# Windowed attention: two of a tile's three weighted rows added on GpSimd before TensorE transposes and sums

## The reference, cut to what matters

```python
kv_c = kv @ w_kv_comp                       # 32 latent channels per key
qc = q @ w_q_down
q_nope, q_rope = (qc @ w_q_up), _rope(qc @ w_q_rope)      # 16 heads x 64 each
k_nope, v = (kv_c @ w_k_up), (kv_c @ w_v_up)
k_rope = _rope(kv_c @ w_k_rope)
scores = (q_nope . k_nope + q_rope . k_rope) * scale
good = (k_idx <= q_seg) & (k_idx >= q_seg - LOOKBACK)     # LOOKBACK = 2
attn = softmax(where(good, scores, neg))
out = attn @ v, heads joined, @ w_out
```

## Time and profile before

| what | us |
|---|---|
| median of 3 runs (lowest, highest) | 1641.42 (1634.97, 1651.33) |
| profiled execution | 1648.7 |
| span of its trace | 1647.0 |
| this phase's steady part, from the first rotation to the end of the tail | 50.20 to 223.77 |

### The profile page before, as it was taken

The page is one execution under the profiler, slowest core; times in us unless marked ns, Lnnn a source line. Parts: engine busy times, 40 slices in busy tenths (PEclk is TensorE's granted clock), DMA queues, the critical chain, the costliest instruction groups (busy, mean ns, idle before and its releaser), DMA issues. The chain is left out here.

```text
span 1647.0 us, 23707 instructions
## 1 busy us (share of the span) xinstructions
PE 1427.8 (87%) x9151; PEld 726.4 (44%) x9151; DVE 982.5 (60%) x1768; ACT 688.9 (42%) x1204; POOL 630.3 (38%) x628
## 2 busy tenths in 40 slices
PE   6868786988989999899968999899999877899984
PEld 3345453333334444444334444444445333355642
DVE  4798948677731222468556774745455344578866
ACT  2444432666642000257534773244433432355522
POOL 1587734354222221333123312534421312356662
PEclk7989997889988999869987998899999978979996
DMA  3000010000020000100001002000000010000000
GB/s 109 0 1 1 1 47 1 1 1 1 1 81 0 1 0 0 53 2 1 11 1 53 2 2 47 1 2 1 1 2 2 2 30 1 7 1 2 2 1 28
DMA packets 17238, 20.65 MB, mean 13 GB/s; under 512 B 7819, under 2 KB 13179, under 8 KB 16488
## 3 DMA queue, kind: packets, MB, share of 16 engines
q1 hardware_dynamic: 17128, 19.13, 3.8%
HBM read 17.94 MB, written 1.05 MB: 12 GB/s over the span
## 5 line engine op out<-in xcount | busy, mean ns | idle before, releaser
L1823 DVE CUSTOM_DVE_ANT_0 P<-P,L2f_mask 128x128 f32<-128x128 f32 (+3 forms) x256 | 118.5, 521 | 105.6 <-PE P L1715 105.6
L1020 DVE TENSOR_REDUCE L0f_nm<-P 128x2 f32<-128x768 f32 (+3 forms) x88 | 97.7, 1120 | 44.4 <-PE P L917 44.1
L1999 PE MATMUL P<-L0m_hm,L0m_w 128*128 128x512 f32 x256 | 113.3, 602 | 0.0
L1793 ACT ACTIVATE L2f_prob<-P 128x1024 f32<-128x1024 f32 x80 | 80.6, 1025 | 74.0 <-PE P L1727 74.0
L974 ACT ACTIVATE L0f_prob<-P 128x512 f32<-128x512 f32 x160 | 87.1, 605 | 39.9 <-PE P L928 38.5
L1634 POOL TENSOR_SCALAR_AFFINE_SELECT L2f_prob<-L2f_prob 128x512 f32<-128x512 f32 x64 | 40.0, 638 | 165.6 <-ACT L2f_prob L1793 165.6
L1715 PE MATMUL P<-L2f_ks,L2f_qs 48*128 48x512 f32 (+3 forms) x512 | 91.8, 471 | 0.3 <-DVE L2f_nm L1823 0.3
L1727 PE MATMUL P<-L2f_qs,L2f_ks 49*128 49x256 f32 (+3 forms) x512 | 84.5, 444 | 3.1 <-DVE L2f_nm L1823 2.3
L2402 POOL TENSOR_TENSOR L3x_exm<-L3x_exm,L3x_rec 128x2048 f32<-128x2048 f32 x16 | 72.4, 4524 | 27.0 <-DVE L3x_rec L2588 27.0
L871 POOL TENSOR_SCALAR_AFFINE_SELECT L0f_prob<-L0f_prob 128x512 f32<-128x512 f32 x64 | 39.9, 638 | 101.9 <-ACT L0f_prob L974 95.0
L1999 PEld LDWEIGHTS P<-L0m_hm,L0m_w 128*128 128x128 f32 x256 | 49.4, 194 | 60.7 <-issue 60.7
(11 more groups left out here) (577 smaller groups left out, 3347.5 us busy)
## 6 DMA issues: line engine op xcount, KB each, us to landing
L0m_w<-in_L0m_w SPq DMA_DIRECT2D x1, 2048.0 KB, 7.9
L0f_va<-in_L0f_va SPq DMA_DIRECT2D x3, 512.0 KB, 4.5
in_xt<-in_x SPq DMA_DIRECT2D x1, 1024.0 KB
L0x_segi<-in_segb SPq DMA_DIRECT2D x1, 1024.0 KB, 5.2
L0m_w<-in_L0m_w SPq DMA_DIRECT2D x1, 1024.0 KB, 9.9
out<-out_o SPq DMA_DIRECT2D x4, 256.0 KB, 2.4
L1x_va<-in_va SPq DMA_DIRECT2D x3, 256.0 KB, 3.2
L1x_vr<-in_vr SPq DMA_DIRECT2D x3, 256.0 KB, 4.1
```

The costliest lines, as they stand in the source:

```text
L1020: nc.vector.tensor_reduce(S.nm[:, qt, first:first + 2 * many].rearrange("p (i e) -> p e i", e=2), P[:, bank:bank + 2, 0:many * width].rear ...
L1793: nc.scalar.activation(S.prob_of(b, g)[:, at:at + 2, :], P[:, bank:bank + 2, :], ACT.Exp).then_inc(*S.act_done.up())
L1823: m = nc.vector.tensor_tensor_reduce(out=at, in0=at, in1=mask[:, T - width:T], scale=1.0, scalar=-3.0e38, op0=ALU.add, op1=ALU.max, accum_ ...
L1999: m = mm(P[:, slot(b, i) + part, :], w1[:, e, part * 512 + i * 128:part * 512 + i * 128 + 128], hm[b % 2][:, e, :], start=e == 0, stop=e = ...
```

## The change

On POOL, L1189 signals a new semaphore `weighed`, POOL waits for it, and adds row 1 of the tile to row 0 in place (128x512); that add now gives the signal for which TensorE and ACT wait. TensorE turns rows 0 and 2 alone: 8 matmuls a tile in place of 12. All three rows are still computed by L1189.

```diff
         ops.tensor_tensor(pv[t % 2][:], kg[b % 3][:, qt, :, 0:32].unsqueeze(2).to_broadcast([128, 3, H, 32]),
-                          p[b % 2][:, qt].unsqueeze(3).to_broadcast([128, 3, H, 32]), ALU.mult)\
+                          p[b % 2][:, qt].unsqueeze(3).to_broadcast([128, 3, H, 32]), ALU.mult).then_inc(*weighed.up())
+        eng.wait_ge(weighed.sem, t + 1)
+        ops.tensor_tensor(pv[t % 2][:, 0], pv[t % 2][:, 0], pv[t % 2][:, 1], ALU.add)\
             .then_inc(*(S.vals_pool if S.pool_has(s) else S.vals_dve).up())
...
+    weighed = ph.count("weighed")
...
                     for g in range(4):
-                        for j in range(3):
+                        for j in (0, 2):
                             m = mm(P[:, bank, g * 128:(g + 1) * 128], pv[(4 * b + n) % 2][:, j, 4 * g:4 * g + 4, :].rearrange("p h c -> p (h c)"),
                                    G["ident"][:], start=j == 0, stop=j == 2)
```

## The result

The changed kernel took 1659.84 us (median of 4 runs, 1655.6 to 1666.95) against 1639.08 us before (4 runs): a ratio of 1.0122, 95% interval 1.0075 to 1.0169. The forecast was a ratio of 1.0124 and 1661.7 us.

A forecast was written before the change was run, and what follows sets the result against it. The prediction took POOL's chain of values through PE's last turn, ACT's copy and exp as the bound; 6.3 + 5.6 + 3.7 + 4.85 = 20.4 us gave a ratio of 1.0124, 1661.7 us, range 1648 to 1671.

The forecast's parts named there:

- The chain: Each step: POOL up to its last value, PE's last turn, ACT's copy, exp, DVE's p, the next step's first value.
- Price of an add: On POOL: 1.27 us for the add plus 0.08 for its wait, 1.35 us; bounds 1.00 and 2.75.
- First step: To the exp at 123.00: four adds, 0.3 us of rotation collision and a longer last turn, +6.3 us (4.7 to 6.4).
- Second step: To the exp at 164.41: 1.0 us of rotation collision, three adds and a longer last turn, +5.6 us (4.05 and 5.75).
- Third step: To the exp at 202.36: three adds, 0.15 of rotation and a longer last turn, less 1.03 us to spare: +3.7 us.
- Tail: From 204.18 on: four values with adds at 4.10 us each, then a last turn of 2.8 us, +4.85 us (4.0 and 5.7).
- the rival with those at the low clock too: TensorE falls to 1.2 GHz in the tail and stays, output matmuls take twice 3.67 us: 25.4 us, 1666.7 us, chance 0.10.
- Sum: Three steps and tail: 6.3 + 5.6 + 3.7 + 4.85 = 20.4 us slower, ratio 1.0124, 1661.7 us.
- The price of the clock: Last turns of 3.5 us in steps and 2.8 in the tail instead of 1.96; rival with clock kept: 15.0 us, chance 0.27.
- DVE's: Rival: DVE is the bound and POOL's holes swallow the adds; only 7 us slower, 1648.4 us, chance 0.09.
- TensorE's turns: Rival: the 16 turns are what is paid, 0.94 us saved on each; 15 us faster, 1626.5 us, chance 0.03.
- Slack: Third step: the exp waited for DVE's softmax, leaving the POOL chain 1.03 us to spare, which the change would use up.

The follow-up runs named there:

- the doubled adds: Changed kernel with every add made twice, each behind a wait for the one ahead: stretch from first value to next phase 180.54 us, ratio 1.027 to the kernel before.
- the add left out: Changed kernel without the add behind the first value of each sequence, TensorE turning three rows of that tile: stretch 152.81 us, against 160.0 in the changed kernel.
- the second trace: Changed kernel measured once more, unchanged: ratio 1.0133 to the kernel before, stretch 160.70 us.
- keeping it up: Changed kernel with useless matmuls in TensorE's gaps: stretch 153.13 us, against 160.0 in the changed kernel.
- leaving them out: Kernel before with no add, TensorE turning rows 0 and 1 alone: stretch 137.39 us, against 138.4 before.
- the run with the add alone: Changed kernel with the add kept but TensorE turning all three rows again: stretch 159.57 us, against 160.0 in the changed kernel.
- the runs with an early exp: exp moved ahead of the copies of turns 2 and 3: stretch 158.74 us (changed kernel), 140.48 (before); with next queries early too, 150.77 and 146.39.
- exp-early version of the kernel: Changed kernel with exp moved from the step's end to behind the last product: stretch 158.74 us, against 160.0 in the changed kernel.

## Why the prediction was right

- **The chain.** POOL from V0 to V3's add, last turn, copy, exp: shown by the timelines, by the doubled adds and by the add left out. In the first step V3's add ended 38.47 us behind V0's start (124.79 + 1.26 - 87.58), forecast 125.2 - 86.36 = 38.84.
- **Price of an add.** 1.27 us, 4.07 with its value (said 1.27 and 4.10).
- **First step.** +5.81, said 6.3: a little less on POOL, and a last turn of 3.41, said 3.5.
- **Second step.** +6.06, said 5.6. The rotation met the add for 0.94 us as said, but the table came 8.84 us behind V0's start in place of 7.49, 1.35 later and not 1.0: the table matmuls behind DVE's add to X took 1.31 us in place of 0.91. And the last turn was 3.68.
- **Third step.** +3.99, said 3.7; a last turn of 3.78. That POOL's products there wait for the rotation (1.89 us, DVE L1389) and no longer for the queries was said as a small 0.15.
- **Tail.** +5.73, said 4.85. The mis-sized term is the last turn, 3.79 us where I took 2.8 as a midpoint. In this trace gaps of 2 us were enough for the clock to fall, and the output matmuls behind the last turn were back at 3.67 us, so the rival with those at the low clock too was too dark here. In the second trace the same gaps left the last turn at 2.55 us and the output matmuls at 6.10. Where in the tail the clock falls is not settled by the gaps alone, and the rows of before could not show it.
- **Sum.** 21.6 us for 20.4. The first step was forecast 0.5 us too long, the other parts 0.5, 0.3 and 0.9 too short, so the errors partly cancel. The price of the clock, 5.5 us of the sum (20.45 - 14.95 before rounding), was measured at 6.8 by keeping it up. That the ratios agree to 0.0002 is luck: the measurement's own interval is 0.5% to either side, and the second one gave 1.0133.
- **The rivals.** Doubling the adds took DVE's, leaving them out took TensorE's turns. What I said of the passes holds at one clock: 16 take 1.95 to 2.05 us at 2.4 GHz where 24 take 2.84 to 2.94. What I did not ask is how 24 passes would have fared behind the same adds; the run with the add alone shows it, and there the clock makes up for all of the extra passes.
- **Slack.** I read from the copy and the exp alone that the last turn leads into the exp; that it also leads through the output matmuls to the next queries I used for the third step only. Two of the forecasts for the runs with an early exp failed on that.

## What to carry to other kernels

Work moved from an engine that waits to one that runs without a hole was paid in full here, whatever the busy shares say: POOL had a lower share than DVE, and each of its adds still cost 1.35 us on the chain. Before counting matmuls as saved, look at what TensorE does in the freed time; here it waited, came back at 1.2 GHz, and a third fewer passes took as long or longer. And read a change of 20 us in the stretch that holds it, since the rest of the program can move by 20 us from one execution to the next.

## What the runs showed of the hardware

The same turns at the same pace do not always keep or lose TensorE's high clock. Turns of 16 passes every 4.07 us, with 2 us between them, took 1.95, 2.05, 2.70 and 3.79 us in the first trace of the changed kernel. In its second trace, from the second turn of the tail on, the fall came later:

```profile
229.60 2.05 PE L1287 MATMUL P<-ident,L0x_pv 128*128 128x128 f32 x16 [2.02 <-POOL L0x_pv L1192]
233.67 2.05 PE L1287 MATMUL P<-ident,L0x_pv 128*128 128x128 f32 x16 [2.02 <-POOL L0x_pv L1192]
237.74 2.55 PE L1287 MATMUL P<-ident,L0x_pv 128*128 128x128 f32 x16 [2.02 <-POOL L0x_pv L1192]
241.06 6.10 PE L1294 MATMUL P<-L0x_on,L0x_wo 128*128 128x512 f32 x8 [0.77 <-ACT L0x_on L1350]
```

In the exp-early version of the kernel the last two turns, behind 2.53 and 2.02 us without work, stayed at 2.05. Turns of 24 passes at the same pace, with 1.13 us between them, kept the clock in the one trace that has them (2.94 us each).

GpSimd's add and a DVE operation with two SBUF inputs held each other up: L1388 took 1.90 us in place of 0.96, and in the same rows the add behind V0 1.46 in place of 1.27. The Trainium skill (SBUF — State Buffer, SBUF: two separate sides) describes an exclusive lock for such a pair, held by the one that starts first for its whole instruction; these rows agree.
